# Two graph layers on one core: projections of the first eight tiles every three quarters, code panels written a panel later, a reordered ramp, and a low part of 256 columns

## The reference

```python
deg = max(row sums of adj, 1)
# layer 0: residual graph convolution, then LayerNorm
pooled = (adj + I) @ x / deg + x          # dinv * a_hat * dinv, both factors of one row
x1 = layernorm(x + relu(pooled @ W0 + b0))
# layer 1: two gates, attention over the neighbours, a graph convolution
h = x1 @ W_sa;  s_l, s_r = h @ a_l, h @ a_r
e = where(adj, exp(-leaky_relu(s_l[:, None] + s_r[None, :], 0.01)), 0)
x_a = e @ h / (row sums of e + 1e-5)
x_b = adj @ (x1 @ W_gcnb) + b_gcnb
gate_a, gate_b = sigmoid([adj @ x1, x1] @ Wa + ba), sigmoid([adj @ x1, x1] @ Wb + bb)
out = layernorm(x1 + sigmoid(gate_a * x_a + gate_b * x_b))
```

## Time and profile before

| what | us |
|---|---|
| median of three runs (876.67 to 878.2) | 876.71 |
| profiled execution, device time | 878.33 |
| its span | 876.2 |
| PE busy | 855.4 (98%) |
| DVE busy | 670.0 (76%) |
| ACT busy | 573.6 (65%) |
| one chunk on DVE, mask / low part (mean of 64) | 2.301 / 2.303 |
| one chunk on ACT: high part (mean of 64); exponentials, 8 of 0.496 | 1.908; 3.3 |

### The profile page before, as it was taken

One profiled execution on the slowest core, in us unless ns is written; L12 is line 12 of the kernel. 1 busy time (PEld: TensorE's weight loads), 2 busy tenths in 40 slices (PEclk: granted clock), 3 DMA queues, 4 the chain that ended last, 5 costly groups with the idle time before them and its releaser, 6 DMA issues.

```text
span 876.2 us, 20454 instructions
## 1 busy us (share of the span) xinstructions
PE 855.4 (98%) x7574; PEld 754.2 (86%) x7574; DVE 670.0 (76%) x1181; ACT 573.6 (65%) x1217; POOL 178.1 (20%) x181
## 2 busy tenths in 40 slices
PE   9999989999999998998899999999999999999997
PEld 7878778888888887887788888888888888888886
DVE  6686756665656468898988988988978978978863
ACT  5765545555555237988977876966966967867831
POOL 1013223222322221012022022032032032032021
PEclk9999999999999999999999999999999999999999
DMA  9889999999989433110220120120120120220001
GB/s 318 271 274 393 328 405 326 360 349 321 378 308 350 167 112 137 56 55 1 79 80 16 62 78 24 54 78 23 55 78 10 67 78 0 78 78 0 25 25 37
DMA packets 66649, 130.01 MB, mean 148 GB/s; under 512 B 5496, under 2 KB 29088, under 8 KB 62112
## 3 DMA queue, kind: packets, MB, share of 16 engines
q1 hardware_dynamic: 57392, 120.61, 38.8%
q10 hardware_dynamic: 9200, 8.64, 2.9%
HBM read 99.87 MB, written 29.36 MB: 147 GB/s over the span
## 4 chain that ended last, share of the span: by engine, by line
PE 81%; DVE 6%; ACT 4%; issue 4%; DMA 2%; POOL 1%; ACTq 0%; POOLq 0%; DVEq 0%; SPq 0%
PE ps L1535 30%; PE ps L1372 23%; PE ps L1476 19%; PE ps L1407 5%; PE ps L1355 3%; DMA strip<-in_adj_dram 2%; DVE ec L1106 2%; ACT ec L629 2%; DVE em L1113 1%; ACT em L638 1%; DVE dd L948 1%; PE ps L1392 1%; PE ps L1340 1%; PE ps L1331 0%; POOL sc L461 0%
## 5 line engine op out<-in xcount | busy, mean ns | idle before, releaser
L1535 PE MATMUL ps<-fb,em 128*128 128x257 f16 x3072 | 347.5, 273 | 0.8 <-DVE em L1113 0.8
L1535 PEld LDWEIGHTS ps<-fb,em 128*128 128x128 f16 x3072 | 300.4, 98 | 38.6 <-issue 1.3
L1372 PE MATMUL ps<-y,codes 128*128 128x257 f16 x2048 | 237.7, 273 | 0.7 <-DVE y L836 0.7
L1372 PEld LDWEIGHTS ps<-y,codes 128*128 128x128 fp8e4 x2048 | 200.4, 98 | 27.7 <-DVE y L836 1.1
L629 ACT ACTIVATE ec<-slb,nsb 128x256 f32<-128x256 f32 x512 | 211.1, 496 | 0.0
L1113 DVE SCALAR_TENSOR_TENSOR em<-ec,em 128x2048 f16<-128x2048 f32 x64 | 147.4, 2303 | 23.7 <-ACT em L638 23.7
L638 ACT ACTIVATE em<-ec 128x2048 f16<-128x2048 f32 x64 | 122.0, 1908 | 65.1 <-PE ps L1535 57.2
L1106 DVE SCALAR_TENSOR_TENSOR ec<-ec,pan 128x2048 f32<-128x2048 f32 x64 | 147.3, 2301 | 2.6 <-issue 1.8
L513 ACT ACTIVATE codes<-strip 128x1024 uint8<-128x1024 f32 x67 | 68.7, 1048 | 34.2 <-DMA strip<-in_adj_dram 33.2
L1476 PE MATMUL ps<-zz,dd 128*128 128x256 f16 x768 | 89.4, 273 | 1.5 <-DVE t L1135 1.3
L461 POOL TENSOR_TENSOR sc<-sc,sc 128x2 f32<-128x2 f32 x15 | 38.5, 2567 | 245.4 <-DVE sc L1215 245.4
(11 more groups left out here) (154 smaller groups left out, 789.0 us busy)
## 6 DMA issues: line engine op xcount, KB each, us to landing
strip<-in_adj_dram SPq DMA_DIRECT2D x128, 512.0 KB, 7.4
a_scratch<-codes SPq DMA_DIRECT2D x16, 1024.0 KB, 10.9
pan<-a_scratch SPq DMA_DIRECT2D x16, 1024.0 KB, 4.8
x_scratch<-x ACTq DMA_DIRECT2D x32, 128.0 KB, 5.2
x1r<-x_scratch SPq DMA_DIRECT2D x16, 256.0 KB, 2.7
h_scratch<-hst ACTq DMA_DIRECT2D x30, 136.0 KB, 4.8
out_dram<-ot SPq DMA_DIRECT2D x15, 256.0 KB, 2.2
fb<-h_scratch SPq DMA_DIRECT2D x3, 1088.0 KB, 8.7
```

Of the source, the lines that this page charges most:

```text
L1372: mm = pe.matmul(ACC(n), codes[:, qq % SLOTS, h, jb, e * P:(e + 1) * P].bitcast(F8), y[:, jb, part, 0:YC], start=(jb == 0 and part == 0), ...
L1535: mm = pe.matmul(PH(2 * m + e)[:, 0:HC], em[:, c, e_part, i, e * P:(e + 1) * P], fb[:, jb, h_part, 0:HC], start=(jb == 0 and e_part + h_pa ...
```

## The change

Five edits, in one kernel:

- `sum_rows`: the low part's product covers 256 columns in place of 257; at the last row block the two parts change places, so that the last product covers all 257. The memset of the low part's 257th column goes.
- `WNORM_AT` is 28 (was 27), which moves the norm and the scales a tile later, and both `weight_parts` follow the last `y_lo` and two casts.
- `t_step(m)` and `p_step(m)` of the first eight tiles (`SPREAD`) come every three quarters of a tile. Before, the projections of tiles 0 to 3 came every two quarters, with a pause of three before tile 4, and then one per tile. From tile 8 on the old places stay. The orders of ACT and DVE around the first eight tiles, and POOL's `g_sums`, are rewritten to suit.
- `CODES_AT`: panel `q` is written to DRAM after strip `16 q + 42`; before, after strip 32 for `q = 0`, 43 for `q = 1` and `16 q + 21` for the others. Panel 6 follows the last strip.
- Layer 1's ramp: in step 1 the copies `low_m34`, `low_m1`, `low_m52` and the DVE reads `middle`, `middle_m1`, `sums_52` come earlier; in step 2 `norm` follows three chunks in place of one, `low_m52` goes from step 2 (step 1 has it), and `middle` moves ahead of `attend`.

```diff
-WNORM_AT = 27
+WNORM_AT = 28
+SPREAD = 8
-            CODES_AT = [2 * GS, 2 * GS + GS // 2 + RING // 2] + [q * GS + GS + RING - 1 for q in range(2, NQ - 1)]
+            CODES_AT = [(q + SLOTS) * GS - RING for q in range(NQ - 2)]
...
+            codes_when_cast(NQ - 2)          # SP, after the last strip
...
-                if n == 3:
-                    g_sums(pool, 0)
-                if n >= 4 and n % 2 == 0:
+                if n < SPREAD and n in (3, 5, 7):
+                    g_sums(pool, (n - 3) // 2)
+                if n >= SPREAD and n % 2 == 0:
                     g_sums(pool, (n - 2) // 2)
...
             cast(7)                          # ACT, first tiles
             x1t_copy(0)
-            cast(2)
+            cast(3)
+            proj_copies(0)
             x1t_copy(1)
-            proj_copies(0)
+            proj_copies(1)
             cast(1)
             x1t_copy(2)
-            proj_copies(1)
             forms_hi(0)
+            cast(2)
+            proj_copies(2)
+            x1t_copy(3)
+            cast(2)
+            proj_copies(3)
+            x1t_copy(4)
             cast(1)
-            x1t_copy(3)
-            proj_copies(2)
-            proj_copies(3)
-            cast(3)
-            for n in range(PT + 2, T + 3):
+            forms_hi(1)
+            cast(2)
+            proj_copies(4)
+            x1t_copy(5)
+            proj_copies(5)
+            x1t_copy(6)
+            forms_hi(2)
+            cast(2)
+            for n in range(SPREAD + 1, T + 3):
...
                 exp_chunk(s + 1, n, 0, nth)  # act_step
                 high_chunk(s, 2)
-                if not ramp:
-                    norm(s - 2, second)
+                if ramp:
+                    low_m34(s + 1)
+                elif second:
+                    high_chunk(s, 3)
+                    low_m67(s)
+                else:
+                    norm(s - 2)
                     low_m52(s)
-                high_chunk(s, 3)
-                if not ramp:
+                if not second:
+                    high_chunk(s, 3)
+                if not ramp and not second:
                     low_m67(s)
                 gates(s, m)
+                if ramp:
+                    low_m1(s + 1)
                 exp_chunk(s + 1, n, 1)
-                if ramp:
-                    low_m34(s + 1)
                 high_chunk(s + 1, 0)
+                if second:
+                    norm(s - 2, second)
                 exp_chunk(s + 1, n, 2)
                 if not ramp:
                     low_m34(s + 1)
                 exp_chunk(s + 1, n, 3)
                 high_chunk(s + 1, 1)
+                if ramp:
+                    low_m52(s + 1)
                 sigmoid(s - 1)
                 gated(s, m)
-                low_m1(s + 1)
+                if not ramp:
+                    low_m1(s + 1)
...
-                if t == T - 1:
-                    weight_parts(0)
             for t in split_at(T):
                 y_lo(t)
             cast(2)
-            weight_parts(1)
+            for part in range(2):
+                weight_parts(part)
             cast(2)
...
+            head(1)                          # DVE, first tiles
+            normalize(1)
+            x1t_lo(0)
+            head(2)
+            normalize(2)
+            h_lo(0)
+            head(3)
+            normalize(3)
+            x1t_lo(1)
+            cast(1)
+            head(4)
+            h_lo(1)
+            normalize(4)
+            cast(1)
+            x1t_lo(2)
             forms_lo(0)
             cast(1)
+            h_lo(2)
+            head(5)
+            normalize(5)
             x1t_lo(3)
+            cast(2)
...
                 if not ramp:                 # dve_step
                     sums_67(s)
                     some_differences(s + 1, n, DIFF_ORDER)
+                if ramp:
+                    middle(s + 1)
                 mask_chunk(s + 1, n, 1)
                 if ramp:
+                    middle_m1(s + 1)
+                low_chunk(s + 1, 0)
+                if second:
                     middle(s + 1)
-                low_chunk(s + 1, 0)
                 attend(s - 1, n, ramp)
                 mask_chunk(s + 1, n, 2)
-                if not ramp:
+                if not ramp and not second:
                     middle(s + 1)
                 low_chunk(s + 1, 1)
-                middle_m1(s + 1)
+                if not ramp:
+                    middle_m1(s + 1)
                 statistics(s - 1)
+                if ramp:
+                    sums_52(s + 1)
                 mask_chunk(s + 1, n, 3)
                 low_chunk(s + 1, 2)
-                sums_52(s + 1)
+                if not ramp:
+                    sums_52(s + 1)
...
-                    for part in range(2):
-                        mm = pe.matmul(ACC(n), codes[:, qq % SLOTS, h, jb, e * P:(e + 1) * P].bitcast(F8),
-                                       y[:, jb, part, 0:YC], start=(jb == 0 and part == 0),
-                                       stop=(jb == T - 1 and part == 1))
+                    for part in ((0, 1) if jb < T - 1 else (1, 0)):
+                        cols = D if part else YC
+                        mm = pe.matmul(ACC(n)[:, 0:cols], codes[:, qq % SLOTS, h, jb, e * P:(e + 1) * P].bitcast(F8),
+                                       y[:, jb, part, 0:cols], start=(jb == 0 and part == 0),
+                                       stop=(jb == T - 1 and part == 0))
...
+            t_quarter = lambda m: 3 * m - 1 if m < SPREAD else 4 * (m - 2)
+            t_after = {t_quarter(m): m for m in range(1, T - 2)}
+            p_after = {t_quarter(m) + 2: m for m in range(T - 2)}
```

More of the change, by code:

```diff
@@ L594, in _ @@
             x1t_copy(0)
-            cast(2)
+            cast(3)
+            proj_copies(0)
             x1t_copy(1)
-            proj_copies(0)
+            proj_copies(1)
             cast(1)
             x1t_copy(2)
-            proj_copies(1)
             forms_hi(0)
-            cast(1)
-            x1t_copy(3)
-            proj_copies(2)
-            proj_copies(3)
-            cast(3)
-            for n in range(PT + 2, T + 3):
-                if n > PT + 2:
-                    proj_copies(n - 3)
+            cast(2)
[4 more added lines that the diff above has]
+            x1t_copy(4)
+            cast(1)
+            forms_hi(1)
[7 more added lines that the diff above has]
+            for n in range(SPREAD + 1, T + 3):
+                proj_copies(n - 3)
                 more = n // PT + 1 < NQ and n < T
@@ L788, in _ @@
             dve.memset(ones[:], 1.0)
-            dve.memset(y[:, :, 0, D:YC], 1.0)
-            dve.memset(y[:, :, 1, D:YC], 0.0).then_inc(S["const_ready"], 1)
+            dve.memset(y[:, :, 0, D:YC], 1.0).then_inc(S["const_ready"], 1)
             def cast(count):
@@ L1004, in head @@
                 stats(n)
[L1006 to L1013, removed]
             head(0)
             normalize(0)
-            first_head(1)
-            first_head(2)
-            first_head(3)
+            head(1)
[13 more added lines that the diff above has]
+            x1t_lo(2)
             forms_lo(0)
             cast(1)
+            h_lo(2)
+            head(5)
+            normalize(5)
             x1t_lo(3)
-            h_lo(2)
+            cast(2)
+            h_lo(3)
+            x1t_lo(4)
             cast(1)
-            head(4)
-            h_lo(3)
-            normalize(4)
+            head(6)
+            forms_lo(1)
+            normalize(6)
             cast(2)
-            for n in range(PT + 2, T + 3):
+            h_lo(4)
+            x1t_lo(5)
+            head(7)
+            h_lo(5)
+            normalize(7)
+            x1t_lo(6)
+            forms_lo(2)
+            cast(2)
+            for n in range(SPREAD + 1, T + 3):
                 more = n // PT + 1 < NQ and n < T
@@ L1038, in _ @@
                     dve.tensor_copy(slc[:], ex[:, :, 2]).then_inc(S["sl_ready"], 1)
-                if PT + 2 < n < T + 2:
+                if n < T + 2:
                     h_lo(n - 3)
@@ L1249, in attend_tile, with dve_step @@
                                   ).then_inc(S["out_ready"], 1)
-            def dve_step(s, m, nth, ramp=False):
+            def dve_step(s, m, nth, ramp=False, second=False):
                 n = 1 - m
@@ L1309, in _ @@
             dve_step(1, 1, 2, ramp=True)
-            dve_step(2, 0, 2)
+            dve_step(2, 0, 2, second=True)
             n0, per_pair = st.n, 2 * 11
@@ L1439, in _ @@
             t_step(0)
-            def sum_tile(n, between):
+            t_quarter = lambda m: 3 * m - 1 if m < SPREAD else 4 * (m - 2)
+            t_after = {t_quarter(m): m for m in range(1, T - 2)}
+            p_after = {t_quarter(m) + 2: m for m in range(T - 2)}
+            for n in range(PT, T):
                 pe.wait_ge(S["stat_ready"], n - PT + 1)
@@ L1445, in sum_tile @@
                     sum_rows(n, i * T // 4, (i + 1) * T // 4)
[L1446 to L1456, removed]
```

(5 more changed lines are left out.)

## The result

The changed kernel takes 871.72 us (median of 5 runs, 869.8 to 872.5) against 878.2 for the kernel before on the same chip (5 runs, 876.67 to 879.72): a ratio of 0.9921, with a 95% interval of 0.9903 to 0.994. That is 6.5 us less, where 12.4 were forecast: the sign is right, the size about half, and the time lies 2.2 us above the range. The profiled execution took 871.72 us with a span of 869.6, against 878.33 and 876.2.

What follows compares the result with a forecast made beforehand. PE was taken as the bound nearly everywhere. Savings of 0.9 (columns), 1.3 (end of Z), 4.9 (first eight tiles), 0 (steady sums) and 5.3 (ramp) sum to 12.4 us: median 864.3, range 862.3 to 869.5.

Steps and rivals of the forecast that it cites:

- Columns: In the sums, 1024 low-part products go from 257 to 256 columns: 0.9 us saved on PE's path.
- End of Z: At the end of Z, moving DVE's scales a tile later removes PE waits: 1.3 us saved, bounds 0.5 and 1.4.
- First eight tiles: Of 6.4 us lost in the first eight tiles, 4.9 saved; projections 1 and 3 still wait 0.7 and 0.6 us.
- a sign that the prediction named for being wrong: A wait (bracket) of PE over 2 us anywhere in its timeline.
- the rival on the code writes: In the steady sums, code writes stop PE at panels 1 to 5, 4.0 us each: 884 us; chance 0.04.
- the first eight tiles wait elsewhere: Strip 31 lands 1.5 us later, so projections 1 and 3 wait over 2 us: 867.6 or 870.9; chance 0.13.
- Ramp: In layer 1's ramp all four PE waits go: 5.3 us saved, bounds 2.5 and 5.55.
- half the ramp comes back: A 2 us slip on DVE or POOL at panels 3 and 4 costs 2.8 us: 867; chance 0.09.
- Steady sums: In the steady sums, writing codes a panel later makes no PE wait: 0 us gained or lost.
- a sign named for being wrong: ACT's waits for strips growing by over 5 us from 126 to 300.
- the rival on the other side: In the steady sums, code writes stall PE at panels 1 to 5, 20 us in all: 884 us; chance 0.04.

Runs made afterwards that it cites:

- run 8: Kernel before with only the end-of-Z edit, `WNORM_AT` 28 and both weight parts behind the cast: 877.92 us, ratio 0.9995.
- run 5: Changed kernel with panels written after strip 16 q + 47, projection 4's copies ahead of casts, low parts ahead of heads, `read_52`'s copy ahead of `norm`: 865.25 us.
- run 4: Changed kernel with ACT's copy for `read_52` ahead of `norm` in layer 1's steady step: 871.08 us, ratio 0.9918.
- run 2: Changed kernel with ACT making projection 4's copies and tile 5's transposed copy ahead of the casts of strips 45 and 47: 867.87 us, ratio 0.9885.
- run 3: Changed kernel with DVE making the low parts of tiles 1 and 3 ahead of the heads of tiles 3 and 5: 872.08 us, ratio 0.9928.
- run 7: Kernel before with only layer 1's reordered ramp (`act_step` and `dve_step`): 873.52 us, ratio 0.9941.
- run 6: Changed kernel with the code writes at their old places, after strips 32, 43 and 16 q + 21: 873.79 us, ratio 0.9941.

## Why the prediction was half right, step by step

**Columns: right.** Transposes 19 tiles apart in PE's timeline, of the kernel before and of the changed kernel:

```profile
152.33 0.38 PE L1392 MATMUL ps<-ident,x 128*128 128x128 f32 x2
...
315.44 0.38 PE L1392 MATMUL ps<-ident,x 128*128 128x128 f32 x2
```

```profile
150.74 0.38 PE L1437 MATMUL ps<-ident,x 128*128 128x128 f32 x2
...
313.35 0.38 PE L1437 MATMUL ps<-ident,x 128*128 128x128 f32 x2
```

A tile repeats after 8.558 us in place of 8.585, 26.7 ns for 32 low-part products, 0.83 ns each and 0.85 us in all; 0.9 was taken from the earlier trace rows. By the Trainium skill's page "TensorE: Matmul & The Clock Gate", section "Back-to-back issue gap", a column is worth 0.42 ns for one matmul by itself; the two traces say twice that, and the measurement decides.

**End of Z: right in its place.** From PE's restart near 21 us to its first sum 35.7 us in place of 37.0, the 1.3 forecast, and 35.7 in run 8 too. But in the times of run 8 no gain is seen, so this can't be taken for 1.3 us of time by itself.

**First eight tiles: the step that failed.** The sentence is "Projections 2, 4, 5 and 6 come out with 0.3 to 3 us to spare." Projections 2, 4 and 6 came without a wait; projection 5 waited 3.02 us, which is also a sign that the prediction named for being wrong. The terms around it were near: projections 1 and 3 were laid with waits of 0.7 and 0.6 and had 1.15 and 0.71; the work is 47.6 (run 5). The prediction had both halves of the cause. It says that the panel which stood before strip 33 now follows strip 42, and it names a cast with a projection's copies behind it, for the old kernel ("ACT's cast 45 the projection's copies") and, in the rival on the code writes, for panels 1 to 5. It shows no steps for projection 5 and does not put the two together for panel 0, whose write falls into the first eight tiles: ACT's new order has the copies of projection 4 and the transposed copy of tile 5 behind the cast of strip 47, and strip 47 behind the panel.

The price of the panel was low as well: 5.5 us on top of a strip's own 1.3, where strip 43 follows strip 42 by 8.1. This is the smaller part. By an estimate from these rows, with 5.5 strip 47 would land at 110.4 in place of 111.75; PE starts 3.4 us behind that landing and stood ready at 112.15, so a wait of 1.7 us would have come out even so. Loss: 53.04 - 47.64 = 5.4 us, where 1.5 was allowed. With -1.0 measured for -4.9, this is 3.9 of the 5.8 us between the spans' changes, -6.6 and -12.4. The rival "the first eight tiles wait elsewhere" had the right kind and the wrong place: strip 31 did come 1.7 us later than laid (cast at 76.88 for 75.2), but PE's own start was 0.95 later too (72.25 for 71.3), and projection 1 waited 1.15. That its price of 4.0 for one wait is near the 3.9 is luck: 1.5 of it stands for a fall of the clock, which did not come in this trace.

**Ramp: right, with one wait underrated.** Measured 4.5 us for 5.3. The rival "half the ramp comes back" named the place, panels 3 and 4; 1.1 us came back, not 2.8. Run 4 shows its cause: `read_52` behind `norm`.

**Steady sums: right that PE does not wait**, though a sign named for being wrong came, ACT's waits growing by over 5 us:

```profile
ACT codes L515 <- DMA strip<-in_adj_dram: 25.1, 12, 4.4
```

ACT's waits for strips from 126 to 300 in the changed kernel, against 13.8, 5 and 4.2 in the earlier trace rows. They nearly doubled and PE has no bracket there. The cover that the prediction named (copies are wanted a tile later) holds; the rival on the other side falls for panels 1 to 5. A late strip on ACT cost 3 us in the first tiles, where a projection comes every 6.8 us, and nothing where it comes every 8.6.

The remaining 1.0 is the start: before's profiled execution happened to have the short wait. The forecast of 864.3 was also counted from a median of 876.71 (three runs), where five runs give 878.2: of the 7.4 us between it and 871.72, 5.9 are the size of the gain and 1.5 this base.

## What to carry to other kernels

When work is packed closer, write down for each in-order engine what stands behind each instruction that waits for a DMA: work that doesn't need the DMA belongs ahead of it (run 2 took the whole wait away with one line moved). A large write put into a queue of reads delays the reads behind it: in the three places tried here (before strips 43, 44 and 48), the next strip lands 6.8 to 8.1 us behind the last one, against some 1.4 without a write. So put it where nothing on the path follows those reads. Mend the last cause first: run 3 removed two waits and won nothing; with the strip behind projection 5 dealt with as well, the stretch fell to 47.64 us (run 5).

## What was not expected of the hardware

The clock after a wait. The changed kernel's PE stood 3.02 us at projection 5 and the granted clock stayed at full level; in run 4 it stood 2.68 us at the same place and the clock fell. Busy time from 110 to 120, first of the changed kernel, then of run 4 (granted clock third from the end):

```profile
110.00:120.00 10.00, 6.98 (x64) 6.00 (x63) 5.60 (x17) 4.61 (x16) 2.91 (x5) 1.00 0.97 349
```

```profile
110.00:120.00 10.00, 7.32 (x56) 5.78 (x54) 4.68 (x15) 5.22 (x18) 2.94 (x5) 0.83 0.90 327
```

It also fell after 2.32 us (before), 2.41 (run 8), 3.27 (run 7), 3.80 (run 6) and 5.09 (run 3), each time for some 3.4 us at 1.2 GHz, in run 3 for twice that. So the length of the wait alone does not tell whether the clock falls; what else does is open. In these traces a fall cost 1.3 to 2.1 us, which is as much as a wait.
